# Two graph attention layers over 4096 nodes: every second unit's codes turned by a transposing transfer, transposes two ahead until slot 9, the end in quarters

## The reference

```python
Af = A + eye(n)
P = softmax(X @ Wq @ (X @ Wk).T + nan_to_num(-inf * (1 - Af)), axis=1)
x = layernorm(x + P @ (X @ Wv))                     # layer 0
h = x @ W.T + b_W
e = (h @ a1)[:, None] + (h @ a2)[None, :] + b_a
e = where(e > 0, e, 0.2 * e)
x = layernorm(x + softmax(where(adj > 0, e, -9e15), axis=1) @ h)   # layer 1
```

## Time and profile before

| what | us |
|---|---|
| median of 3 runs | 253.81 (253.43 to 254.62) |
| the profiled execution | 255.0 |
| its span, first to last instruction | 253.2 |
| PE busy in the span | 236.2 |
| DVE, ACT, POOL busy | 185.3, 154.4, 61.4 |

### The profile page before, as it was taken

One profiled execution on the slowest core, in us unless ns is written; L12 is line 12 of the kernel. 1 busy time (PEld: TensorE's weight loads), 2 busy tenths in 40 slices (PEclk: granted clock), 3 DMA queues, 4 the chain that ended last, 5 costly groups with the idle time before them and its releaser, 6 DMA issues.

```text
span 253.2 us, 4017 instructions
## 1 busy us (share of the span) xinstructions
PE 236.2 (93%) x1523; PEld 133.3 (53%) x1523; DVE 185.3 (73%) x284; ACT 154.4 (61%) x182; POOL 61.4 (24%) x104
## 2 busy tenths in 40 slices
PE   5959999499999999999999999999999999999980
PEld 4947675245555555555555555555555555555450
DVE  1378787967777777779768776977777778797433
ACT  2468978989067999170489994610899982220032
POOL 3284688999200000003030000002300000032122
PEclk9999999679999999999999999999999999999998
DMA  6999999999999999999589999998499920010102
GB/s 187 365 386 389 383 387 383 387 387 386 385 388 383 380 384 387 387 386 385 64 237 305 332 403 392 387 387 298 114 299 339 397 99 3 1 41 3 41 3 88
DMA packets 40939, 71.76 MB, mean 283 GB/s; under 512 B 5843, under 2 KB 6100, under 8 KB 40916
## 3 DMA queue, kind: packets, MB, share of 16 engines
q1 hardware_dynamic: 40480, 71.33, 79.2%
q10 hardware_dynamic: 436, 0.13, 0.2%
HBM read 69.36 MB, written 2.10 MB: 282 GB/s over the span
## 4 chain that ended last, share of the span: by engine, by line
PE 86%; POOL 3%; ACT 3%; DMA 2%; DVE 2%; issue 2%; ACTq 1%; POOLq 0%; DVEq 0%
PE banks L1202 67%; PE banks L1158 10%; PE banks L1217 3%; PE banks L1095 3%; DMA brow<-in_L_gnn_b_W_dram 2%; ACT a L737 2%; PE banks L1110 1%; POOL rstd L597 1%; PE banks L1081 1%; DVE y L1036 0%; POOL f_parts L636 0%; POOL xhat_st L602 0%; POOL frstd L646 0%; POOL feat L629 0%; DVE e_sb L938 0%
## 5 line engine op out<-in xcount | busy, mean ns | idle before, releaser
L1202 PE MATMUL banks<-e_sb,f_parts 128*128 128x512 f16 x768 | 186.1, 391 | 1.5 <-DVE e_sb L938 1.1
L926 DVE SCALAR_TENSOR_TENSOR e_sb<-R,cr_word,banks 128x1024 f32<-128x1024 f32 x124 | 153.8, 1275 | 30.9 <-PE banks L1158 28.3
L737 ACT ACTIVATE a<-a_sb,code_bias 128x2048 fp8e4<-128x2048 int32 x64 | 124.3, 1997 | 2.8 <-DMA a_sb<-in_adj_dram 2.1
L1202 PEld LDWEIGHTS banks<-e_sb,f_parts 128*128 128x128 f16 x768 | 71.6, 97 | 86.8 <-issue 4.0
L646 POOL TENSOR_TENSOR frstd<-frv,minus_half 128x4 f32<-128x4 f32 x8 | 8.1, 1012 | 168.9 <-DVE frv L962 167.6
L1158 PE MATMUL banks<-ident,a 128*128 128x128 f16 x496 | 38.0, 220 | 3.6 <-ACT a L737 3.6
L1158 PEld LDWEIGHTS banks<-ident,a 128*128 128x128 f16 x496 | 32.8, 98 | 15.4 <-ACT a L737 3.9
L728 ACT COPY R<-banks 128x512 f32<-128x512 f32 x8 | 4.7, 587 | 35.9 <-PE banks L1110 35.9
L753 ACT ACTIVATE junk<-y 128x128 f32<-128x128 f32 x28 | 8.3, 298 | 26.8 <-DVE y L953 26.8
L944 DVE RECIPROCAL rden<-banks 128x4 f32<-128x4 f32 x7 | 1.3, 183 | 12.2 <-PE banks L1217 12.2
L1095 PEld LDWEIGHTS banks<-m0c_um,x_tr 128*128 128x128 f32 x64 | 9.6, 224 | 0.8
(11 more groups left out here) (113 smaller groups left out, 101.9 us busy)
## 6 DMA issues: line engine op xcount, KB each, us to landing
a_sb<-in_adj_dram SPq DMA_DIRECT2D x64, 1024.0 KB, 12.4
x_sb<-in_x_dram SPq DMA_DIRECT2D x8, 256.0 KB, 9.9
out_dram<-out_sb SPq DMA_DIRECT2D x8, 256.0 KB, 5.8
w_nat<-in_L_gnn_W_dram ACTq DMA_DIRECT2D x1, 64.0 KB, 3.2
wv<-in_L_gnn_Wv_dram ACTq DMA_DIRECT2D x1, 64.0 KB, 3.1
acol<-in_L_gnn_a_vec_dram SPq DMA_DIRECT2D x1, 1.0 KB, 3.0
bcol<-in_L_gnn_b_W_dram ACTq DMA_DIRECT2D x1, 0.5 KB, 4.5
ba<-in_L_gnn_b_a_dram ACTq DMA_DIRECT2D x1, 0.0 KB
```

The lines of the kernel that those rows point to most:

```text
L737: nc.scalar.activation(a8[:, n % 2, Q * h:Q * (h + 1), k * PW:(k + 1) * PW], a_parts[:, m % SLOTS, :, :], ACT.Relu, bias=code_bias[:, :], ...
L926: nc.vector.scalar_tensor_tensor(out=e_sb[:, k % NE, :], in0=R[:, g % 2, :], scalar=cr_word[:, 0, 2 * t + b:2 * t + b + 1], in1=ps_code[s ...
L1202: ins = nc.tensor.matmul(ps_acc[g % 2][h][:, :], f[:, j, :], e_half[:, k % NE, cols, part], start=(j == 0 and n == 0), stop=(j == T - 1 an ...
```

## The change

- Units 17, 19, ..., 63 (`by_dma`) are not turned by PE. Right behind their codes, ACT issues a transposing transfer (`move`) from the codes in SBUF to one of `NM` = 4 buffers in SBUF, which are the old `x_tr`. DVE's `edges` waits for it (`at_landed`) and reads the codes there. ACT's codes of two chunks later wait for it too. Counts of PE's turned units and their banks go by `turned(s)`.
- The codes are written so that the words of a unit stand side by side in `a8` (1024 words of two bytes for each partition); ACT's `codes` therefore writes pairs of bytes in two places, and PE's `turn` reads contiguous words.
- PE turns two ahead (behind the sums) until slot `LATE` = 9 instead of 4, and there `turn(slot + 3)` too.
- `last_sums` takes the second half in two quarters: columns 512 to 767 of the three units, then 768 to 1023. The last quarter of units 61 to 63 is summed in a bank of its own (`ps_last`) and added by a DVE instruction to what ACT has copied.
- Head: SP loads `adj`'s first part ahead of x's block 1; ACT makes codes 0 ahead of `copy_xt(1)`; PE does `weights(1)` and `layer0(0)` ahead of `x_turned(1)`, without four filler matmuls; POOL does `features(0, 0)` ahead of `root(1)`; DVE does `words(0)` ahead of its wait for `root(1)`.

```diff
+        def by_dma(s):
+            return s >= U and s % 2 == 1
+        def moved_to(eng, s):
+            d = moved(s)
+            eng.wait_ge(at_landed[d % NM], 16 * (d // NM + 1))
 # SP
                 load_x(0)
                 sp.dma_start(acol[:, :], a_cols, allow_slow_non_contiguous=True).then_inc(avec_loaded, 16)
+                load(0)
                 load_x(1)
-                load(0)
 # POOL
                 root(0)
+                features(0, 0)
                 root(1)
-                features(0, 0)
 # ACT
                     if n >= 2:
-                        act.wait_ge(at_ready, 4 * (n - 2) + 2 * (k + 1))
-                    nc.scalar.activation(a8[:, n % 2, Q * h:Q * (h + 1), k * PW:(k + 1) * PW],
-                                         a_parts[:, m % SLOTS, :, :],
+                        before = 4 * (n - 2) + 2 * (k + 1)
+                        act.wait_ge(at_ready, turned(before))
+                        if by_dma(before - 1):
+                            moved_to(act, before - 1)
+                    nc.scalar.activation(a_words[:, n % 2, k, :, h, :, :].rearrange("p e x b -> p x e b"),
+                                         a_parts[:, m % SLOTS, :, :].rearrange("p q (w e b) -> p (q w) e b", e=2, b=2),
+                def move(s):
+                    n, c = divmod(s, 4)
+                    d = moved(s)
+                    act.wait_ge(codes_ready, PARTS * n + 2 * (c // 2) + 2)
+                    if d >= NM:
+                        act.wait_ge(p_ready, 2 * (moved_unit(d - NM) + 1))
+                    else:
+                        act.wait_ge(y0_ready, QUADS)
+                    nc.scalar.dma_start_transpose(out=at_moved[d % NM], in_=a16[:, n % 2, c // 2, c % 2, :]).then_inc(
+                        at_landed[d % NM], 16)
                 copy_xt(0)
-                copy_xt(1)
                 act.wait_ge(consts_ready, 12)
                 codes(0)
+                copy_xt(1)
                         codes(slot + CODES_AHEAD)
+                        if by_dma(slot + CODES_AHEAD):
+                            move(slot + CODES_AHEAD)
 # DVE
                 divide(0, inner)
+                words(0)
                 dve.wait_ge(rstd_ready, 2)
                 divide(1, scores)
-                words(0)
                 words(1)
+                    if k == 0:
+                        dve.wait_ge(half_done, 3)
+                        dve.wait_ge(acc_copied, 2 * G)
+                        nc.vector.tensor_tensor(acc_t[:, LAST:GW], ps_last[:, :], acc_t[:, LAST:GW],
+                                                ALU.add).then_inc(acc_copied, 1)
 # PE
                 def turn(s):
+                    if by_dma(s):
+                        return
@@ last_sums
                     ins.then_inc(half_done, 1)
+                    pe.wait_ge(r_ready, 2 * G)
                     for k in range(2):
-                        pe.wait_ge(acc_copied, 2 * G + k)
-                        projections(1, quad(4), range(2 * k, 2 * k + 2)).then_inc(fin_mm, 1)
+                        for s in units:
+                            if s == S - 1:
+                                if k == 0:
+                                    pe.wait_ge(acc_copied, 2 * G - 1)
+                                    pe.wait_ge(y_ready, 2 * G - 2)
+                                    projections(0, quad(0), range(Q)).then_inc(fin_mm, 1)
+                                else:
+                                    pe.wait_ge(acc_copied, 2 * G)
+                                    projections(1, quad(4), range(2)).then_inc(fin_mm, 1)
+                            for b in range(2):
+                                ins = products(s, b, (slice(HW, LAST), slice(LAST, GW))[k])
+                        ins.then_inc(half_done, 1)
+                    pe.wait_ge(acc_copied, 2 * G + 1)
+                    projections(1, quad(4), range(2, 4)).then_inc(fin_mm, 1)
@@ head and slots
                 weights(0)
+                weights(1)
+                layer0(0)
                 x_turned(1)
-                weights(1)
-                keep_busy(bank[0], 4)
-                layer0(0)
                 layer0(1)
...
-                    if FIRST < slot < S - NA:
+                    if LATE < slot < S - NA:
                         turn(slot + NA)
...
-                    if slot <= FIRST:
+                    if slot <= LATE:
                         turn(slot + 2)
-                    if slot == FIRST:
+                    if slot == LATE:
                         turn(slot + 3)
```

More of the change, by code:

```diff
@@ L49, in graph_layers @@
     HW = GW // 2
+    LAST = GW - 2 * P
     U = 16
@@ L59, in graph_layers @@
     NE = 8
+    NM = 4
     CODES_AHEAD = 4
@@ L144, in graph_layers @@
         x_tr = sb("x_tr", [P, 4, Q * P])
+        at_moved = [x_tr[:, i, :].bitcast(F16).rearrange("p (r n) -> p r n", r=TG) for i in range(NM)]
+        code_moved = [x_tr[:, i, :].bitcast(F8).rearrange("p (n b) -> p n b", b=2) for i in range(NM)]
         acc_t = sb("acc_t", [P, GW])
@@ L220, in graph_layers @@
         at_ready = sem("at_ready")
+        at_landed = [sem(f"at_landed{i}") for i in range(NM)]
         p_half = sem("p_half")
@@ L244, in wait_xhat, with moved, turned, moved_unit @@
                 eng.wait_ge(xhat_later, i - 1)
+        def by_dma(s):
+            return s >= U and s % 2 == 1
+        moved_units = [s for s in range(S) if by_dma(s)]
+        turned_units = [s for s in range(S) if not by_dma(s)]
+        def moved(s):
+            return sum(m < s for m in moved_units)
+        def turned(s):
+            return sum(m < s for m in turned_units)
+        def moved_unit(d):
+            return moved_units[d]
+        def turned_unit(m):
+            return turned_units[m]
+        def moved_to(eng, s):
+            d = moved(s)
+            eng.wait_ge(at_landed[d % NM], 16 * (d // NM + 1))
         def group_at(slot, offset):
@@ L792, in _ @@
                 nc.scalar.copy(acc_t[:, 0:HW], ps_acc[g % 2][0][:, :]).then_inc(acc_copied, 1)
+                act.wait_ge(half_done, 2)
+                nc.scalar.copy(acc_t[:, HW:GW], ps_acc[g % 2][1][:, :]).then_inc(acc_copied, 1)
                 squares(g, 0)
-                act.wait_ge(half_done, 2)
-                for k in range(2):
-                    cols = slice(k * HW // 2, (k + 1) * HW // 2)
-                    nc.scalar.copy(acc_t[:, HW:GW][:, cols], ps_acc[g % 2][1][:, cols]).then_inc(acc_copied, 1)
                 act.wait_ge(frv_ready, 2 * g)
@@ L1193, in sums, with products @@
                         pe.wait_ge(p_ready, 2 * s + b + 1)
-                        products(s, b, 0)
-                        products(s, b, 1).then_inc(mm_done, 1)
-                def products(s, b, h):
+                        products(s, b, halves[0])
+                        products(s, b, halves[1]).then_inc(mm_done, 1)
+                def products(s, b, cols):
                     g, t = divmod(s, U)
                     k, j = 2 * s + b, 2 * t + b
-                    cols = slice(h * HW, (h + 1) * HW)
+                    h, first = divmod(cols.start, HW)
+                    dst, opened = ps_acc[g % 2][h][:, first:first + cols.stop - cols.start], j == 0
+                    if cols.start == LAST:
+                        dst, opened = ps_last[:, :], k == 2 * (S - HALVED)
                     for n, (f, part) in enumerate(((fl, 1), (fh, 1), (fh, 0))):
-                        ins = nc.tensor.matmul(ps_acc[g % 2][h][:, :], f[:, j, :], e_half[:, k % NE, cols, part],
-                                               start=(j == 0 and n == 0), stop=(j == T - 1 and n == 2))
+                        ins = nc.tensor.matmul(dst, f[:, j, :], e_half[:, k % NE, cols, part],
+                                               start=(opened and n == 0), stop=(j == T - 1 and n == 2))
                     return ins
```

42 lines of the change are left out of this document (23 added, 19 removed).

## The result

The changed kernel takes **405.73 us** (median of four runs, 405.19 to 408.2) against 254.22 for the kernel before on the same chip: a ratio of 1.597 [1.593, 1.601]. The forecast was 240.6, with a range to 253.0. The profiled execution has a span of 404.3 us at a mean granted clock of 0.853.

A forecast was written before the change was run, and what follows sets the result against it. The prediction took PE, busy 93%, as the bound, with memory traffic not far behind. Terms of -10.75, -6.5, +2.8, +1.5 and -0.25 sum to -13.2 us, so 253.8 becomes 240.6 us, range 235.5 to 253.

The forecast's parts named there:

- Part 2 (b): ACT's queue: issue time of a transfer (I) taken as 1.0 us, beside 35.0 us a group; no cost up to 2.0.
- ACT's issues are long: Rival: next codes wait behind issues on ACT's queue; 264 us at 3.0 us an issue, slower than before; chance 0.10.
- Part 1: Transposes of 24 units leave PE: -10.75 us; DVE's edges reading codes from SBUF taken as unchanged.
- Part 2 (a): DMA engine time of one transfer (T): taken as 1.0 us, between 0.68 and 1.28; hidden up to 1.07.
- the first rival: The load stream becomes the bound, at 1.07 to 1.65 us of engine time per transfer: 246 to 253 us; chance 0.17.
- Part 2 (c): Landing of a transfer before DVE's edges: 3 to 6 us on its own queue, hidden; queued like loads, 5 lost.
- Part 3: PE turning two ahead until slot 9 removes the pause at 44 us and slow stretch: -6.5 us, bounds -6.6 and -4.
- Part 4: Reordered head: POOL's order delays the first products, +2.8 us (0 to 3.5); falling clock, +1.5 (0 to 2.7).
- the head costs nothing: Rival: the reordered head adds no time, 236.3 us; chance 0.10.
- Part 5: Last sums' second half in quarters at the kernel's end: -0.25 us, bounds -1 and +0.7.
- Cut small: Rival: transfers go in small pieces, over 1.65 us of engine time each; 342 us at 5.5; chance 0.06.
- Serial blocks: Rival: a transfer's eight blocks go one after the other, 3.1 us each; 686 us in all; chance 0.02.

The follow-up runs named there:

- x2: Kernel before with only the codes written in two-byte pairs to two places, all units turned on PE: 356.63 us, ratio 1.40.
- x1: The whole change, but ACT reads its input in pairs and writes the codes in long runs: 257.12 us, ratio 1.012.
- x8: x1 with the old head, 24 units still moved by transfer: 248.92 us, ratio 0.980.
- x6: x1 with the old head and no unit moved by transfer: 249.09 us, ratio 0.983.
- x4: Kernel before with only PE's turning two ahead until slot 9: 249.48 us, ratio 0.981.
- x10: x8 with ACT 6 units ahead of PE's slot instead of 4 from slot 9: 251.26 us, ratio 0.990.
- x7: x1 with the old head and 12 units moved, every fourth: 243.67 us, ratio 0.958.
- x12: x10 with 16 units moved instead of 24: 243.25 us, ratio 0.958.
- x5: Kernel before with only the new head: 261.05 us, ratio 1.027.
- x9: Kernel before with ACT and DVE write-pattern probes and four transfers without loads added at its end; ran once; transfers took 1.37 us of all engines each.

## Why the prediction was wrong

**The step that failed is Part 2 (b), and in it the term "16 codes of 1.91".** The sum for ACT's group took the codes at the price of the earlier trace rows although the change rewrote their output pattern. Measured are 4.85 each, so 16 x 2.94 = 47 us more: 35.0 becomes 82, and with the issue at its 1.53 and the 0.1, 8 more of them make 95 us a group against PE's 49.6. By the formula of that step the cost is 3 x (95 - 49.6) - 7.5 = 129 us, of the 165 between forecast and result. The formula starts at unit 16; the codes before it are slow as well. x2 shows the term alone: ACT's busy time rises by 171 us, from 154.4 to 325.6, on a kernel where ACT had 99 us to spare, and the time by 102. What after has beyond x2, 49 us, is argued and not shown to be mostly the 24 issues in the same queue (24 x 1.53 = 37 us; ACTq has 8% of the chain, 32 us), since on a kernel bound by ACT little hides them; the rest was not taken apart.

With this one term put right the forecast would still be low. x1 takes 257.1, 16.5 us above it and outside the range: 10.6 are what the 24 transfers lose (x8, below), 3.9 the head beyond its 4.3 (8.2 in x1 less x8), and some 2 are what x6 falls short of parts 3 and 5.

The pattern was seen, as an aside in the rival *ACT's issues are long*: "0.7 us more on each of the 16". The direction was right and the size four times too small, 2.9 in place of 0.7; at 2.9 the rival's own measure (1.4 of I per 0.7) gives 5.9, far beyond its I = 2.6 for "slower". So the rival that came true had a chance of 0.10, for another main reason. Every added operation got two bounds, and the changed access pattern of an existing one got none in the sum, though no row of the trace showed it.

**Part 1** was right. DVE's edges read from SBUF take 1280 ns against 1275 from PSUM in the same run (1288 against 1270 in x8), and 12 units moved gave 5.4 us, at 0.45 each. The transposes that now read contiguously take 219 ns in the mean in x6, as in x4, and 0.45 us for eight. DVE's slack was 17% per instruction by the part's own numbers ((49.6 - 3.5) / 39.5), not 20; nothing hangs on it.

**Part 2 (a), T.** Taken 1.0, measured 1.37 in quiet, beyond the upper working bound of 1.28. In the runs the queue's share gives much the same: in x1 12.6% of 255.5 us less about 0.5 of other packets is 31.7, or 1.32 each; the others lie between 1.30 (x10) and 1.55 (x7), where loads run beside them. With T = 1.37 the part's formula gives 23 x 1.37 - 24.7 = 6.8 us for 24 units, so the engines decide, as the first rival said. For 12 and 16 units it gives 16.4 and 21.9 us against 24.7, no cost, and x7 and x12 show none. x8 lost 10.6 us against what the removed transposes should bring (249.1 - 10.75 = 238.3). That its engines are full is shown; that 6.8 of the loss is their time and the remaining 3.8 the waits of (b) and (c) is argued: no run changed the size of the loads alone.

**Part 2 (b), I.** Taken 1.0; 1.25 to 1.36 in quiet, 1.25 in the median in x7, 1.68 to 1.76 in the median and 3.3 to 3.5 at most in x1 and x8. The median stays under the threshold of 2.0, and the cost was hidden in x7. With 24 moved ACT waited 24.6 us in the issues' wake.

**Part 2 (c), the landing.** Estimated at 3 to 6 us "on a queue of its own", measured 12.4 to 12.6 in x1 and x8 beside loads at 12.4 to 15.9, 7.3 beside loads at 6.3, and 3.2 alone. A queue of its own did not shield it. The text priced that case at 5 us in all, at group starts; DVE's waits in x8, 20 of them and 35.3 us, say it comes at nearly every moved unit. What it costs by itself is not shown: x10 halved these waits and the time did not fall.

**Part 3** was right in mechanism, and its size within its bounds. -6.5 predicted, with slot 10 ending at 63.4. From `sums(4)` to the spread of slot 11, x4 takes 24.9 us against 31.1, so 6.2 gained. Its median falls only by 4.9; in the profiled execution 1.3 us of head are in between, with a clock that rose later. Nor does the kernel before lose the same to its clock in every execution: in x4's round the kernel before took 252.05 us at a mean granted clock of 0.993 and 254.69 at 0.976. At 249.48 x4 is nearer to the expectation's "codes or features bind" (249 to 254) than to its 247.3, but the pause is gone and POOL's features hold the first of these products for 0.47 us, against 0.48 before.

**Part 4** was right in mechanism, under in size: +4.3 predicted, with bounds that add to 6.2, +6.5 measured in x5. POOL's order binds as described. The walk had block 1 turned by 11.4 and layer 0 of it done at 13.6; x5 has the block awaited until 10.78, and that layer ending at 14.8. Features 0 came at 16.98 instead of 15.8 and the products at 22.31 instead of 20.8: each step 1 to 1.5 us late. The start of the products is 4.3 us later than before; the other 2.2 of the 6.5 are put down to the clock, granted at 0.71 and 0.72 in 18 to 24 and 24 to 30 us, where before had 1.00 in both. That the pause of 3.7 us did this is not shown: x4, with the old head and a pause of 1.07, had 0.74 in the first of the two, and 1.00 in the second. The rival *the head costs nothing* falls. x1 and x8 differ by this head alone, 257.1 and 248.9: with units moved it costs 8.2.

**Part 5**: -0.25 predicted, nothing gained. From the start of the last products to the end of the last y the chain takes 247.11 + 0.61 - 233.24 = 14.48 us before, and in x6, where the same stretch begins and ends with the first and last of these pieces:

```profile
226.63 8.14 PE banks L1270 x42
...
239.03 0.43 DVE acc_t L1094
...
240.47 0.61 DVE y L1097 x2
```

which is 241.08 - 226.63 = 14.45. One pair of y less is left at the end, and the 0.43 us add, which now has to come between the last products and their projection, takes most of that back.

**The remaining rivals.** Cut small: no. 1056 packets a transfer, near the 1024 rows of 256 bytes of the middle case. Serial blocks: no; eight blocks land in 3.2 us together. The Trainium skill's page "VectorE: DVE Perf Modes" (The three transpose paths) gives 1309 ns for one block by DMA; as an estimate, eight of them one after the other would be 10.5 us, and the quiet landing of 3.2 speaks against multiplying it so. The Trainium skill's page "Advanced Engine Details and Errata" (X-Bar Transpose (TRN2)) expects 350 to 400 GB/s, where the 1.37 us of x9 are 0.262 MB / 1.37 = 191 GB/s; the trace disagrees, by half.

## What to carry to other kernels

A rewritten access pattern is a new operation: price it with bounds from both sides even if the instruction, its shape and its types stay. When ACT must permute a layout in passing, put the jumps on the side that is read (2.09 us here) and let the output be written in runs of at least 4 bytes or steadily onward (4.82 us otherwise). Before moving work to transfers, count the time that the DMA engines have left: here 12 to 16 transfers fitted and 24 did not, and a wait cured by issuing earlier came back on the issuing engine.

## What the runs showed of the hardware

- ACT and DVE pay for output that alternates between places in runs under 4 bytes: with runs of two one-byte values 4.83 us for 2.00 on ACT and 2.73 for 1.21 on DVE, and 9.3 on ACT with one element a run. Read with the same jumps, ACT's input costs 0.09 us alone, and 2.13 against 2.00 in the kernel.
- A transposing transfer of 256 KB takes 1.37 us of all sixteen engines (x9), twice its bytes at the loads' 386 GB/s, and holds ACT's queue for at least 1.25 us.
- It landed 3.2 us after its issue began with no load beside it (x9), 7.3 beside loads that took 6.3 (after), and 12.4 beside loads that took 15.9 (x8), though it has a queue of its own.
- The same pause of 1.07 us ahead of the first six products was followed by 1.52 us of them in one execution and by 2.72 in another (x4). What decides it was not settled.
